# Sending the last batch's rows to the expert slots in one stream instead of in rounds of three

## The chip, the cores and the metric

The kernel runs on one core of one Trainium2 chip. The metric is the device time of one execution in microseconds (us), the median of several runs. Engines go by these names: PE is TensorE (PEld its weight loads), ACT is ScalarE, DVE is VectorE, POOL is GpSimd, SP is SyncE, which here only issues DMAs.

## What is computed

Four batches of 1024 tokens with 128 features go through four layers, each added to its input:

```
x = x + attn_a(layernorm(x))     # linear attention with exponential features, and an FFN
x = x + ffn(layernorm(x))        # mixture of experts (stages named m)
x = x + attn_b(layernorm(x))     # causal softmax attention, 16 heads of width 8
x = x + ffn(layernorm(x))        # the same mixture of experts again (stages named n)

def ffn(x):                      # 160 experts, the best 8 of each token, width 64
    top_w, top_idx = top_k(sigmoid(x @ router_w.T + bias), 8)
    h = silu(x @ w_gate[e].T)            # for each chosen expert e
    y = h @ w_down[e].T                  # weighted by top_w, summed over the 8
    return y + silu(x @ w_gate_shared.T) @ w_down_shared.T
```

## The kernel before, in words

A mixture layer works through DRAM. A router stage (`route`) finds for every token its 8 experts and for each of the 8 a slot. A slot is a row of the DRAM tensor `slots_in`. The rows are then sent there ("scattered"): one indirect DMA issued by POOL (line 859, in the class `Scatter`) sends 128 rows of 128 floats, for one tile of 128 tokens and one of the 8 choices. The 32 tiles of tokens are two halves of 16 tiles, each half with slots of its own, so a half needs 128 scatters. The expert stage (`experts`) reads the slots in order, computes, and writes `slots_out`. POOL then fetches the results back with indirect DMAs of the same size (line 884, class `Gather`), and DVE weighs and adds them.

The expert stage handles the two halves one after the other. A half has 52 groups of 8 blocks with 64 slots each. For one group, SP loads 256 KB of rows (line 1306), PE turns them (`psX`, line 1364, 4 matmuls), ACT copies them (`xT`, line 1409), PE does the first product (`psH`, line 1377, 16 matmuls), ACT squashes it (`hT`, line 1415), PE does the second product (`psY`, line 1388, 16 matmuls), ACT copies the result (`y`, line 1421, and adds 1 to the semaphore `y_ready`), and SP stores 256 KB (line 1311). PE's order is: `psH` of group n, `psX` of n+1, `psY` of n-1. ACT's is `hT` of n, `xT` of n+1, `y` of n-1. DVE copies expert weights into a ring of four buffers (`staged_w`, line 1446) for 32 of the 52 groups, each once `psY` has freed a buffer. Rows and results have rings of four buffers (`DEEP`).

The scatters of the first half are all done before the expert stage begins. Those of the second half are not: in the first expert stage (m) the 64 of the last batch are left, in the second (n) 70, which are those and the last 6 of the batch before. POOL sends them while PE and ACT compute the first half. The helper `spaced` ties them to the groups: three scatters, then a wait until ACT has written `y` of two more groups, then three more, and so on. The first three wait for nothing. When all are issued, POOL waits until they have landed and until the first half's results are stored, and then gathers the first half's results during the second half, again through `spaced`, two gathers for each group. SP begins to load the second half when the first half's stores are issued and the scatters of the second half have landed (semaphores `scattered`).

Of the kernel before, what the change touches and what calls it, by code (L numbers as in the profile page):

```python
# [41 lines left out]
EXPERTS, TOPK, INTER = 160, 8, 64  # L42
# [5 lines left out]
TPH = TILES // HALVES  # L48
# [816 lines left out]
class Gather:  # L865
# [12 lines left out]
    def issue(self, pool, count):  # L878
        for n in range(self.asked, self.asked + count):
            i, k = divmod(n, TOPK)  # L880
            t = self.first + i
            if k == 0 and i >= self.ring:
                pool.wait_ge(self.added, i - self.ring + 1)
            self.nc.gpsimd.indirect_dma_start(self.rows(i)[:, k, :], None, self.G.slots_out[t // TPH],  # L884
                                              bass.IndirectOffsetOnAxis(self.G.place[:, t, k:k + 1], 0)
                                              ).then_inc(self.gathered[i % self.ring], 16)
        self.asked += count
# [390 lines left out]
def experts(nc, stage, G, S, scatter, out=None):  # L1278
# [3 lines left out]
    with Memory(nc, stage) as m:  # L1282
# [10 lines left out]
        src, dst = ([s.rearrange("(g p j) d -> g p (j d)", p=P, j=TURNS) for s in slots] for slots in (G.slots_in, G.slots_out))  # L1293
        order = group_order()
        dynamic_at = [i for i, (_, d) in enumerate(order) if d is not None]
        rows_landed = [m.sem(f"rows_landed{i}") for i in range(DEEP)]
        stored = [m.sem(f"stored{i}") for i in range(DEEP)]
# [4 lines left out]
        @block.sync  # L1302
        def _(sp):
            def load(h, i):
                n = h * HALF_GROUPS + i
                sp.dma_start(rows[:, n % DEEP, :, :].rearrange(flat), src[h][order[i][0]]).then_inc(rows_landed[n % DEEP], 16)

            def store(h, i):
                n = h * HALF_GROUPS + i
                sp.wait_ge(y_ready, n + 1)  # L1310
                sp.dma_start(dst[h][order[i][0]], y[:, n % DEEP, :, :].rearrange(flat)).then_inc(stored[n % DEEP], 16)  # L1311

            for h in range(HALVES):
                for b in range(BPH * h, BPH * (h + 1)):
                    sp.wait_ge(S.scattered[b], 16 * TPB * TOPK)
                for i in range(DEEP):
                    load(h, i)
                for i in range(HALF_GROUPS):
                    if i + DEEP < HALF_GROUPS:
                        sp.wait_ge(x_turned, h * HALF_GROUPS + i + 1)  # L1320
                        load(h, i + DEEP)
                    store(h, i)
            for s in stored:
                sp.wait_ge(s, 16 * HALVES * HALF_GROUPS // DEEP)
            if out is not None:
                for b in range(BATCH):
                    sp.wait_ge(gather.added, TPB * (b + 1))
                    sp.dma_start(out[b].rearrange("(t p) d -> p t d", p=P), G.x[:, b, :, :]).then_inc(out_stored, 16)
                sp.wait_ge(out_stored, 16 * BATCH)

        @block.gpsimd
        def _(pool):
            def spaced(issue, count, first, transfers, groups):

                for n in range(0, count, transfers):
                    done = min(n // transfers * groups, HALF_GROUPS)
                    if done:
                        pool.wait_ge(y_ready, first + done)
                    issue(min(transfers, count - n))

            spaced(scatter, TPH * TOPK - scatter.sent, 0, 3, 2)
            for s in S.scattered[BPH:]:
                pool.wait_ge(s, 16 * TPB * TOPK)
            for s in stored:
                pool.wait_ge(s, 16 * HALF_GROUPS // DEEP)
            spaced(lambda count: gather.issue(pool, count), min(TPH, gather.tiles) * TOPK, HALF_GROUPS, 2, 1)
            if out is not None:
                for s in stored:
                    pool.wait_ge(s, 16 * HALVES * HALF_GROUPS // DEEP)
                gather.issue(pool, TPH * TOPK)  # L1350
# [84 lines left out]
        @block.vector  # L1435
        def _(dve):
            def stage_weights(h, d):
                _, e = nc.values_load_multi_w_load_instructions(
                    G.tile_expert[0:1, h, GROUP * d:GROUP * (d + 1)], engines=[mybir.EngineType.DVE], min_val=0, max_val=EXPERTS - 1,
                    skip_runtime_bounds_check_because="the plan clamps it to the last expert")  # L1440
                if d >= STAGED:
                    dve.wait_ge(down_done, h * HALF_GROUPS + dynamic_at[d - STAGED] + 1)
                elif h:
                    dve.wait_ge(down_done, (h - 1) * HALF_GROUPS + dynamic_at[DYN_GROUPS + d - STAGED] + 1)
                for j in range(GROUP):
                    last = nc.vector.tensor_copy(staged_w[:, d % STAGED, j, :],  # L1446
                                                 G.wgd[:].rearrange("p e i -> p (e i)")[:, bass.ds(e[j] * (INTER + DM), INTER + DM)])
                last.then_inc(staged, 1)

            for c in range(CHUNKS):  # L1450
                dve.wait_ge(S.weights_landed[c], 16)
            for d in range(DYN_GROUPS):
                stage_weights(0, d)
            done = 0
            for d in range(DYN_GROUPS):
                stage_weights(1, d)
                if d % 3 == 2 and d >= 2 * STAGED:
                    gather.add(dve, done)
                    done += 1
            for i in range(done, gather.tiles):  # L1460
                gather.add(dve, i)
# [974 lines left out]
```

## Time and profile before

| | us |
|---|---|
| median of 3 runs | 2910.31 (2908.22 to 2914.45) |
| the profiled execution | 2888.6 |
| its span, first to last instruction | 2887.3 |
| PE busy | 1992.7 (69%) |
| DVE busy | 1664.6 (58%) |
| POOL busy | 1306.3 (45%) |
| ACT busy | 1049.6 (36%) |
| scatters, line 859, 512 of them | 503.8 busy |
| gathers, line 884, 512 of them | 508.5 busy |

The profile is of one execution. Starts are counted from the beginning of the span. The two expert stages together are a little over a fifth of the span: stage m runs from about 983 to 1318 us, stage n from about 2328 to 2672 us.

### The profile page before, as it was taken

The page shows a single profiled execution, that of the slowest core. Times are in us where ns is not written, and L with a number is a line of the kernel's source. Part 1 is how long each engine was busy: PE and PEld are TensorE (multiplying, and loading weights), DVE is VectorE, ACT ScalarE, POOL GpSimd, SP SyncE. Part 2 cuts the span into 40 slices and gives each one's busy share as a digit, 9 for nine tenths or more (in the row PEclk, how much of TensorE's full clock was granted, in tenths as well). Part 3 has the DMA queues.
Part 4 walks back from the last instruction along what each step waited for, and adds up shares of the span by engine and source line. Part 5 has one row for each costly group of instructions (what it writes and reads, how often), then busy time and mean ns, then how long its engine had stood idle before and what let it go on. Part 6 is the DMA issues. An engine that isn't in the chain of part 4 may idle for free. (4 is left out here: it accounts for less than half of the span.)

```text
span 2887.3 us, 45561 instructions
## 1 busy us (share of the span) xinstructions
PE 1992.7 (69%) x15787; PEld 1142.0 (40%) x15787; DVE 1664.6 (58%) x4731; ACT 1049.6 (36%) x2016; POOL 1306.3 (45%) x1340
## 2 busy tenths in 40 slices
PE   5896696696696577664878788987988657766000
PEld 3455355255355355452333333433333335554000
DVE  5466566657567533355786787688785443245222
ACT  0253253253253245442355544434444234443000
POOL 0042265365465343554345540551454634356775
PEclk9898798698798599887687786787787679788555
DMA  9200000000003466664222121211200556565221
GB/s 378 86 1 4 15 15 23 22 18 20 28 16 158 154 209 202 193 189 144 53 70 65 50 64 25 60 54 43 58 32 23 207 191 209 189 194 179 72 60 46
DMA packets 132475, 275.69 MB, mean 95 GB/s; under 512 B 29411, under 2 KB 44387, under 8 KB 127891
## 3 DMA queue, kind: packets, MB, share of 16 engines
q1 hardware_dynamic: 99478, 205.60, 21.6%
q0 software_dynamic: 32768, 67.17, 7.7%
q8 instruction: 127, 2.08, 0.3%
q14 instruction: 102, 0.84, 0.1%
HBM read 146.34 MB, written 125.93 MB: 94 GB/s over the span
## 5 line engine op out<-in xcount | busy, mean ns | idle before, releaser
L859 POOL DMA_INDIRECT slots_in<-g_xs,g_place x512 | 503.8, 984 | 462.8 <-issue 119.3
L2199 ACT ACTIVATE b_pT<-b_psE 128x512 f32<-128x512 f32 (+3 forms) x768 | 326.6, 490 | 452.9 <-PE b_psE L2096 399.4
L1896 DVE TENSOR_REDUCE b_peak<-b_psM 128x1 f32<-128x512 f32 (+3 forms) x768 | 393.3, 550 | 145.0 <-PE b_psM L2084 88.2
L884 POOL DMA_INDIRECT r_xs<-slots_out,g_place x336 | 334.9, 997 | 226.8 <-ACT b_pT L2199 96.6
L2079 PE MATMUL b_psM<-b_kS,b_qS 72*128 72x512 bf16 (+3 forms) x640 | 242.4, 391 | 58.5 <-DVE b_peak L1896 33.0
L2096 PE MATMUL b_psE<-b_qS,b_kS 75*128 75x512 bf16 (+3 forms) x768 | 245.2, 397 | 44.5 <-ACT b_pT L2199 39.4
L884 POOL DMA_INDIRECT g_xs<-slots_out,g_place x176 | 173.6, 987 | 138.2 <-issue 46.4
L2108 PE MATMUL b_psV<-b_pT,b_vb 128*32 128x512 f32 (+3 forms) x1536 | 207.1, 622 | 23.9 <-POOL b_pT L2263 22.0
L1446 DVE COPY m_staged_w<-wgd 128x192 f32 x512 | 98.3, 264 | 203.6 <-PE m_psY L1388 113.0
L1446 DVE COPY n_staged_w<-wgd 128x192 f32 x512 | 97.1, 261 | 204.4 <-PE n_psY L1388 144.0
L2263 POOL TENSOR_SCALAR_AFFINE_SELECT b_pT<-b_pT 128x512 f32<-128x512 f32 x128 | 82.3, 643 | 206.9 <-ACT b_pT L2199 205.3
L2079 PEld LDWEIGHTS b_psM<-b_kS,b_qS 72*128 72x128 bf16 x640 | 69.8, 111 | 212.2 <-DVE b_peak L1896 131.6
L2096 PEld LDWEIGHTS b_psE<-b_qS,b_kS 75*128 75x128 bf16 x768 | 76.4, 111 | 156.7 <-ACT b_pT L2199 88.7
L2082 PE MATMUL b_psM<-b_kS,b_qS 72*128 72x128 bf16 x512 | 130.6, 255 | 8.3 <-DVE b_peak L1896 5.8
L2084 PE MATMUL b_psM<-b_mask_q,b_ident_bf 128*128 128x128 bf16 x512 | 131.4, 257 | 0.0
L417 PE MATMUL a__psA<-a_wk,a_xnT 128*128 128x512 f32 x128 | 67.8, 656 | 45.7 <-POOL a__v L378 45.7
L1364 PE MATMUL m_psX<-g_ident,m_rows 128*128 128x128 f32 x416 | 80.8, 325 | 25.8 <-issue 19.7
L1364 PE MATMUL n_psX<-g_ident,n_rows 128*128 128x128 f32 x416 | 80.9, 326 | 25.0 <-issue 18.9
L611 DVE TENSOR_REDUCE a__shift<-a__sq 128x16 f32<-128x1024 f32 x32 | 39.0, 1220 | 88.4 <-ACT a__sq L536 88.4
L385 POOL TENSOR_TENSOR a__fold<-a__sq 128x512 f32<-128x512 f32 x32 | 41.8, 1305 | 105.4 <-ACT a__sq L556 105.4
L1421 ACT ACTIVATE n_y<-n_psY 128x512 f32<-128x512 f32 x104 | 62.3, 601 | 72.8 <-DMA b_qS<-b_negp 40.2
L1409 ACT ACTIVATE m_xT<-m_psX 128x512 f32<-128x512 f32 x104 | 62.0, 597 | 69.3 <-PE m_psX L1364 62.4
(518 smaller groups left out, 4221.4 us busy)
## 6 DMA issues: line engine op xcount, KB each, us to landing
wgd<-in_w_gdT SPq DMA_DIRECT2D x8, 3840.0 KB, 23.0
slots_in<-g_xs SPq DMA_DIRECT2D x26, 1024.0 KB
m_rows<-slots_in SPq DMA_DIRECT2D x104, 256.0 KB
slots_out<-m_y SPq DMA_DIRECT2D x104, 256.0 KB
n_rows<-slots_in SPq DMA_DIRECT2D x104, 256.0 KB
slots_out<-n_y SPq DMA_DIRECT2D x104, 256.0 KB
b_qS<-q_parts SPq DMA_DIRECT2D x48, 192.0 KB
b_kS<-k_parts SPq DMA_DIRECT2D x48, 192.0 KB
```

The lines of the kernel that those rows point to most:

```text
L859: self.nc.gpsimd.indirect_dma_start(self.G.slots_in[self.h], bass.IndirectOffsetOnAxis(self.G.place[:, TPH * self.h + t, k:k + 1], 0), sel ...
L884: self.nc.gpsimd.indirect_dma_start(self.rows(i)[:, k, :], None, self.G.slots_out[t // TPH], bass.IndirectOffsetOnAxis(self.G.place[:, t, ...
L1364: last = nc.tensor.transpose(psX[:, n % 2, j * P:(j + 1) * P], rows[:, n % DEEP, j, :], G.ident[:])
L1446: last = nc.vector.tensor_copy(staged_w[:, d % STAGED, j, :], G.wgd[:].rearrange("p e i -> p (e i)")[:, bass.ds(e[j] * (INTER + DM), INTER ...
L1896: nc.vector.reduce_max(to, taking()[:, 0:size], AX.X).then_inc(m_taken, 1)
L2079: last = nc.tensor.matmul(ps[:, 0:edge], qS[0:STACK, g, h, qt * P:(qt + 1) * P], kS[0:STACK, g, h, kh * HALF:kh * HALF + edge], start=True ...
L2082: nc.tensor.matmul(ps[:, edge:n], qS[0:STACK, g, h, qt * P:(qt + 1) * P], kS[0:STACK, g, h, kh * HALF + edge:kh * HALF + n], start=True, s ...
L2084: last = nc.tensor.matmul(ps[:, edge:n], ident_bf[:], mask_q[:], start=False, stop=True)
L2096: nc.tensor.matmul(psE[:, j % BANKS, q0:HALF], kS[0:STACK + 3, g, h, kt * P:(kt + 1) * P], qS[0:STACK + 3, g, h, half * HALF + q0:(half + ...
L2108: last = nc.tensor.matmul(psV[32 * h:32 * h + 32, half, q0:HALF], vb[:, kt, g * HG + h, :], pT[:, e % KEPT, h, q0:HALF], start=(kt == 0), ...
L2199: nc.scalar.activation(pT[:, e % KEPT, h, q0:HALF], psE[:, j % BANKS, q0:HALF], ACT.Exp, scale=SCALE).then_inc(e_taken, 1)
L2263: nc.gpsimd.affine_select(out=tile, in_=tile, compare_op=ALU.is_ge, fill=0.0, base=0, pattern=[[0, HG], [1, P]], channel_multiplier=-1).th ...
```

## The change

The call of `spaced` for the scatters is replaced by one call of the scatter itself with the full count. POOL issues the remaining scatters one behind the other, with no wait on `y_ready` between them. Everything else stays, the paced gathers too.

```
-            spaced(scatter, TPH * TOPK - scatter.sent, 0, 3, 2)
+            scatter(TPH * TOPK - scatter.sent)
             for s in S.scattered[BPH:]:
                 pool.wait_ge(s, 16 * TPB * TOPK)
```

## Rows read from the trace of the kernel before

**Rows 1.** The page: busy time by engine, and the chain that ended last, by engine.
```profile
PE 1992.7 (69%) x15787; PEld 1142.0 (40%) x15787; DVE 1664.6 (58%) x4731; ACT 1049.6 (36%) x2016; POOL 1306.3 (45%) x1340
...
PE 7%; POOL 5%; issue 3%; ACT 1%; another core or an unknown queue 1%; DMA 0%; DVE 0%; POOLq 0%; SPq 0%; ACTq 0%; DVEq 0%
```

**Rows 2.** Windows, scatters alone: stretch, length, POOL busy (count), PE clock, DMA share, GB/s.
```profile
999.20:1119.30 120.10, 57.90 (x60) 0.91 0.65 208
1119.30:1138.00 18.70, 0.96 (x1) 1.00 0.68 229
...
2342.60:2474.80 132.20, 64.70 (x66) 0.91 0.65 211
```

**Rows 3.** Timeline, one round of three in stage n: start, length, engine, line [idle before].
```profile
2372.56 0.97 POOL L859 DMA_INDIRECT slots_in<-g_xs,g_place  x1 [2.40 <-ACT n_y L1421]
...
2373.05 0.67 PE L1388 MATMUL n_psY<-n_staged_w,n_hT 64*64 64x128 f32 x16
...
2373.80 0.69 PE L1377 MATMUL n_psH<-n_xT,n_staged_w 128*64 128x64 f32 x16
...
2375.11 0.97 POOL L859 DMA_INDIRECT slots_in<-g_xs,g_place  x1 [0.30 <-issue]
2375.34 0.60 ACT L1421 ACTIVATE n_y<-n_psY 128x512 f32<-128x512 f32 x1 [1.59 <-DMA b_qS<-b_negp]
...
2376.97 0.38 ACT L1415 ACTIVATE n_hT<-n_psH 128x256 f32<-128x256 f32 x1 [1.03 <-DMA b_kS<-k_parts]
...
2378.60 1.05 POOL L859 DMA_INDIRECT slots_in<-g_xs,g_place  x1 [2.52 <-ACT n_y L1421]
```

**Rows 4.** Timeline, ACT in stage m after its last scatter.
```profile
1120.81 0.60 ACT L1421 ACTIVATE m_y<-m_psY 128x512 f32<-128x512 f32 x1 [0.22 <-PE m_psY L1388]
...
1131.84 0.60 ACT L1421 ACTIVATE m_y<-m_psY 128x512 f32<-128x512 f32 x1
```

**Rows 5.** Timeline, where the first halves begin and end, stages m and n.
```profile
983.46 0.96 POOL L859 DMA_INDIRECT slots_in<-g_xs,g_place  x1 [19.49 <-POOLq L93]
...
1137.13 1.16 ACT L1421 ACTIVATE m_y<-m_psY 128x512 f32<-128x512 f32 x2 [0.23 <-PE m_psY L1388]
...
2328.83 0.97 POOL L859 DMA_INDIRECT slots_in<-g_xs,g_place  x1 [19.84 <-POOLq L93]
...
2332.03 1.11 PE L1364 MATMUL n_psX<-g_ident,n_rows 128*128 128x128 f32 x4 [18.87 <-issue]
...
2333.83 1.13 PE L1377 MATMUL n_psH<-n_xT,wgd 128*64 128x64 f32 x16 [0.69 <-ACT n_xT L1409]
...
2483.67 1.16 ACT L1421 ACTIVATE n_y<-n_psY 128x512 f32<-128x512 f32 x2 [0.23 <-PE n_psY L1388]
```

**Rows 6.** Windows, two cycles of gathers: gathers alone on POOL, then `n_y` alone on ACT.
```profile
2588.49:2595.10 6.61, 3.83 (x4) 1.00 0.64 201
2606.28:2616.49 10.21, 5.78 (x6) 0.82 0.49 149
...
2588.49:2595.10 6.61, 1.21 (x2) 1.00 0.64 201
2606.28:2616.49 10.21, 1.20 (x2) 0.82 0.49 149
```

**Rows 7.** Timeline, inside and behind the six gathers in a row.
```profile
2607.14 0.69 PE L1377 MATMUL n_psH<-n_xT,n_staged_w 128*64 128x64 f32 x16
...
2612.63 0.96 POOL L884 DMA_INDIRECT g_xs<-slots_out,g_place  x1 [0.30 <-issue]
2614.87 0.38 ACT L1415 ACTIVATE n_hT<-n_psH 128x256 f32<-128x256 f32 x1 [4.45 <-DMA b_kS<-k_parts]
```

**Rows 8.** Timeline, router stage of batch 3, between scatters sent back to back.
```profile
936.02 1.94 PE L1014 MATMUL m__ps_lo<-g_ident,g_xs 128*128 128x128 f32 x8 [16.39 <-DVE g_xs L1101]
936.16 0.96 POOL L859 DMA_INDIRECT slots_in<-g_xs,g_place  x1 [0.30 <-issue]
937.14 0.60 ACT L1078 ACTIVATE m__xnT<-m__ps_lo 128x512 f32<-128x512 f32 x1 [25.14 <-PE m__ps_lo L1014]
```

## Prediction, made before the changed kernel was run

> **What bounds the kernel now.** I read the page first, for who is busy and who is in the chain that ended last. No engine is busy throughout: PE has 69%, POOL 45%, and the chain as far as the profile can follow it is PE 7% and POOL 5% [rows 1]. So the answer depends on the stage, and the change touches only the first half of the two expert stages. Next I took the scatters by windows. Between the first scatter that waits for a group and the last, stage m has 60 scatters in 120.1 us and stage n 66 in 132.2 us [rows 2]. That is 20 and 22 rounds of three, two groups a round, so both stages run at 6.0 us a round, 3.0 us a group. POOL is busy for less than half of it (57.90 of 120.1) and waits for ACT the rest: POOL does not pace the groups by its own work, and DMA is at 0.65 of its time. The usual conclusion would be that PE and ACT set the pace and that the scatters are hidden.
>
> The timeline says otherwise. After stage m's last scatter, `y` starts at 1120.81 and, five groups later, at 1131.84, with loads and stores still going: 11.03 / 5 = 2.2 us a group [rows 4]. At full clock PE's three blocks of a group are about 0.66 us each (0.67 and 0.69 in the round shown [rows 3]), near 2.0 us together, so a group without scatters is set by PE and takes 2.0 to 2.2 us. I use **2.1 us**. With three scatters in every 6.04 us (2372.56 to 2378.60 [rows 3]) two groups take 6.04 instead of 4.2 us, so a round costs **1.84 us**, 0.61 us a scatter.
>
> Where it is lost can be seen in one round [rows 3]. `psY` is through at 2373.05 + 0.67 = 2373.72, but the `y` that needs it starts at 2375.34, 1.6 us later, with ACT idle. `psH` is through at 2374.49, and its `hT` starts at 2376.97, 2.5 us later and 0.9 us after the third scatter ended (2375.11 + 0.97 = 2376.08). The releasers printed there, DMAs of the attention layer, can't be meant: those tensors are out of use in this stage. What ACT waits for by the code is PE's semaphores. So while POOL issues scatters, PE's results reach ACT late. The trace shows that and not its mechanism.
>
> **The change, part by part.** It removes the waits on `y_ready`, 21 in stage m and 23 in stage n. It moves no other instruction: POOL has nothing queued behind the scatters except the waits for landing and storing and then the gathers, which need the first half's stores anyway. SP's wait for `scattered` before the second half is met earlier, and it was met in time before. It adds nothing. So nothing can be gained on POOL or SP, and what is left is how the same scatters, packed into one stream, slow PE and ACT.
>
> A scatter in a row takes 0.97 + 0.30 = 1.27 us [rows 3]. Stage m's 64 are a stream of 81 us, stage n's 70 one of 89 us. PE starts 3.2 us after the first scatter (2328.83 to 2332.03 [rows 5]), so three scatters cost nothing, now as then. That leaves 61 + 67 = 128 scatters beside running groups.
>
> What one of them costs in a stream is the number that decides. No scatter stream beside running groups is in the trace; the nearest rows are longer bursts of gathers in the second half, DMAs of the same size from the same queue. Four in a row: two groups in 6.61 us, 6.61 - 4.2 = 2.4 us lost, 0.60 each. Six in a row: two groups in 10.21 us, 6.0 us lost, 1.0 each [rows 6]. From three to six in a row the loss rises from 1.84 to 6.0 us, 1.39 us for each added one, which is more than the 1.27 us that it lasts. In the long burst `psH` was through at 2607.83 and `hT` started at 2614.87, 7 us later and 1.3 us after the burst's end (2612.63 + 0.96) [rows 7]. So the gap behind a burst is when PE's results get through, and a stream has no gap. Bounds for the loss per scatter are 0.60 us (as in short bursts) and 1.27 us (groups stand still). I take **1.05 us**, near the six in a row, a little above as there is no pause in 61.
>
> The Trainium skill says the opposite of these rows: in "SBUF — State Buffer", section "Who interferes with whom", PE and ACT never wait on anyone and DMA never contends with a compute engine. By that rule a scatter costs the groups nothing, neither in rounds nor in a stream.
>
> Stage m: the stream ends 81 us after its first scatter, and results get through 1 us later. PE has had 82 - 3 = 79 us, less 61 x 1.05 = 64 us, so 15 us, 7 groups. The other 45 take 45 x 2.1 = 94.5 us. I add 2 us for the last group's way through ACT and for a PE clock that comes back from its lower level (16 `psH` matmuls take 1.13 us at the start of a stage [rows 5] and 0.69 at full clock). Sum: 82 + 94.5 + 2 = 178.5 us. Before it is 983.46 to 1138.29, 154.8 us [rows 5]. **Plus 23.7 us.**
>
> Stage n: 89 + 1 = 90 us, PE has 87 - 67 x 1.05 = 16.5 us, 8 groups; the other 44 take 92.4 us; 90 + 92.4 + 2 = 184.4 us. Before it is 2328.83 to 2484.83, 156.0 us [rows 5]. **Plus 28.4 us.**
>
> The second halves, with the gathers, stay as they are, only later. The sum is +52 us on the profiled execution's 2888.6 us, 2941 us. The median shown, 2910.3 us, is 21.7 us above that execution; I put the same difference on it: **2962 us**.
>
> **The rivals.**
>
> *The same loss per scatter.* Each scatter costs 0.61 us, wherever it stands. For it: four in a row cost 0.60 each, like three. Against it: the six. Then stage m has done 20 groups by the stream's end (79 - 61 x 0.61 = 42 us) and stage n 22, and the end comes at 82 + 32 x 2.1 + 2 = 151 and 90 + 30 x 2.1 + 2 = 155 us, 4 and 1 us under before: about 2905 us, a measured "no change" (the bound of what can be told from no change is 0.2%, 5.8 us).
>
> *The scatters cost nothing.* Something else makes the rounds 6 us long, and taking the waits out changes nothing: 2910 us. For it: POOL is far from busy, and in the router stage PE's first four transposes are through near 936.99 (half of the 1.94 us) and ACT starts on them at 937.14, 0.15 us later, in the middle of scatters sent back to back [rows 8]. So a stream alone doesn't hold PE back; the groups' many small matmuls or SP's loads must have part in it. Against it: the pace turns from 3.0 to 2.2 us a group at the last scatter, in the same stage. The rule cited above from the Trainium skill, "SBUF — State Buffer", would give this case.
>
> *A loss per burst, faster.* The loss is charged once for every burst, not for every scatter, as when PE's signals are held up only at a burst's start. It decides if a stream costs less than about 0.6 us a scatter. Three and four in a row cost 1.84 and 2.4 us, which is not far from a constant; the six speak against it. With 42 rounds gone and two bursts in their place, 40 x 1.84 = 74 us go: 2836 us. Half-way to it, at 0.5 us a scatter, it is 128 x 0.11 = 14 us under the equal case, near 2890 us.
>
> *Standstill.* Each scatter costs its whole 1.27 us: 82 + 52 x 2.1 + 2 = 193 and 201 us, +38 and +45, 2993 us; with 2.2 us a group another 10 us, 3003 us.
>
> **How the numbers follow.** Slower by my mechanism, from 0.75 us a scatter to standstill: 0.69. The same loss per scatter or none: 0.13. Faster, by the loss per burst or a part of it: 0.18. A loss of 0.75 is 38 us under the sum at 1.05, so the likeliest case has 2924 to 3003 us of its own, its middle 2962. The range takes in the equal cases and the half-way fast one and stops short of the pure loss per burst: 2888 to 3000 us. Slower by over 0.2%: 0.70, within 0.2%: 0.11, faster: 0.19.
>
> **What would show each step.** Right: 64 and 70 scatters back to back at 1.27 us from 983 and 2329 us; some 7 or 8 `y` while they last, `hT` starting several us after its `psH`; low DMA share and probably a lower PE clock there; afterwards 2.1 us a group; the first halves 178 and 184 us long. Wrong: more than 20 `y` beside each stream (the loss is smaller), or a pace after the stream far from 2.1 us, as when the loads at 256 KB in and out for every group become the bound. Wrong in another way: DVE's copies of weights could stretch scatters beyond 1.27 us, and a stream of 90 us would grow.

## The result and the profile after

The changed kernel is slower. Its four executions took 2989.42 to 3004.28 us, median 2998.59; the four of the kernel before 2908.22 to 2915.16, median 2912.38. The ratio is 1.0278, 95% interval 1.0254 to 1.0301, or +86 us. I had said 2962 us, in a range of 2888 to 3000. The sign was right, and so was the mechanism, that scatters in a stream hold back PE's results. The size was the one that I had priced as "standstill" (2993 us).

The page of the changed kernel (execution of 2989.42 us), busy time and the chain by engine, to hold against [rows 1]:

```profile
PE 1984.4 (66%) x15787; PEld 1133.0 (38%) x15787; DVE 1664.4 (56%) x4731; ACT 1055.4 (35%) x2016; POOL 1297.1 (43%) x1340
...
PE 5%; POOL 5%; another core or an unknown queue 5%; issue 2%; ACT 1%; DMA 1%; DVE 0%; POOLq 0%; SPq 0%; ACTq 0%; DVEq 0%
```

Every engine is busy for as long as before, within 10 us. Between the two profiled executions the span grew by 100.8 us, all of it time in which the engines are idle, and the page alone doesn't say where. The windows do. First stage m's first half in three stretches with all engines (the stream, the time from its end to the first `y`, the rest), then `m_y` alone on ACT in the same stretches, then stage n's stream, scatters alone on POOL. The columns are length, busy (count) by engine, PE clock, DMA share, GB/s:

```profile
984.92:1065.41 80.49, 9.02 (x78) 6.48 (x79) 6.74 (x32) 2.56 (x5) 61.28 (x64) 0.52 0.20 68
1065.41:1074.95 9.54, 2.65 (x11) 1.30 (x11) 0.00 (x0) 0.00 (x0) 0.00 (x1) 0.50 0.02 7
1074.95:1178.48 103.53, 95.41 (x1787) 70.50 (x1786) 45.61 (x253) 79.16 (x151) 0.00 (x0) 0.97 0.75 248
...
984.92:1065.41 80.49, 0.00 (x0) 0.52 0.20 68
1065.41:1074.95 9.54, 0.00 (x0) 0.50 0.02 7
1074.95:1178.48 103.53, 31.07 (x52) 0.97 0.75 248
...
2377.63:2466.45 88.82, 67.79 (x70) 0.50 0.20 66
```

PE does 78 matmuls in 80 us where it needs 36 for each group, and there is no `y` at all in the stream nor in the 9.5 us behind it. Then all 52 follow in 103.5 us. Stage n repeats it. The next rows show ACT in m from the start, and the two ends of the first halves, to hold against [rows 4, 5]:

```profile
989.38 0.60 ACT L1409 ACTIVATE m_xT<-m_psX 128x512 f32<-128x512 f32 x1 [35.25 <-issue]
1002.02 0.38 ACT L1415 ACTIVATE m_hT<-m_psH 128x256 f32<-128x256 f32 x1 [12.04 <-remote]
1005.57 0.60 ACT L1409 ACTIVATE m_xT<-m_psX 128x512 f32<-128x512 f32 x1 [3.17 <-DMA a_proj<-in_projT]
1045.50 0.38 ACT L1415 ACTIVATE m_hT<-m_psH 128x256 f32<-128x256 f32 x1 [39.33 <-remote]
1056.70 0.60 ACT L1409 ACTIVATE m_xT<-m_psX 128x512 f32<-128x512 f32 x1 [10.82 <-DMA a_proj<-in_projT]
1074.95 0.60 ACT L1421 ACTIVATE m_y<-m_psY 128x512 f32<-128x512 f32 x1 [17.65 <-remote]
...
1177.17 1.16 ACT L1421 ACTIVATE m_y<-m_psY 128x512 f32<-128x512 f32 x2 [0.23 <-PE m_psY L1388]
...
2578.90 1.16 ACT L1421 ACTIVATE n_y<-n_psY 128x512 f32<-128x512 f32 x2 [0.23 <-PE n_psY L1388]
```

So m's first half lasts from 984.92 to 1178.33, 193.4 us in place of 154.8, and n's from 2377.63 to 2580.06, 202.4 us in place of 156.0. That is 38.6 + 46.4 = 85 us, the whole difference of the medians. The second halves are 6.3 and 5.3 us longer in this trace as well; in the runs below, which leave the gathers as they are, they vary by as much without the stream, so I don't put that on the change.

The same stage on PE shows how it stands still. These rows are from the first half's third group, at the stream's end:

```profile
1057.35 1.12 PE L1377 MATMUL m_psH<-m_xT,wgd 128*64 128x64 f32 x16 [43.00 <-issue]
...
1061.59 0.37 PE L1364 MATMUL m_psX<-g_ident,m_rows 128*128 128x128 f32 x1 [3.12 <-issue]
...
1063.69 0.37 PE L1364 MATMUL m_psX<-g_ident,m_rows 128*128 128x128 f32 x1 [1.73 <-issue]
1064.46 0.95 POOL L859 DMA_INDIRECT slots_in<-g_xs,g_place  x1 [0.31 <-issue]
```

The four transposes of `psX`, which at this clock are otherwise one piece of 1.12 us, come one at a time, two or more us apart, and the profile gives nothing that they wait for. The 9.5 us behind the stream are of the same kind: a backlog of PE that drains after the last scatter.

But most of the time goes by between PE's records and its signals. The second group's `psH` and the first group's `psY` are recorded early in the stream:

```profile
1006.22 1.12 PE L1377 MATMUL m_psH<-m_xT,wgd 128*64 128x64 f32 x16 [14.03 <-issue]
...
1008.32 1.15 PE L1388 MATMUL m_psY<-wgd,m_hT 64*64 64x128 f32 x14
```

The `hT` that needs this `psH` starts at 1045.50, 38 us after the recorded end, and the `y` that needs this `psY` at 1074.95. PE's records run ahead: 34 matmuls and 34 weight loads within 3.3 us from 1006.22 on, and only then singly. So the 78 matmuls above are not results that ACT could use. Whether the array really did the work at the recorded time and only the signal was late, or the work itself was, the profile can't tell, as it models the ends of matmuls.

### The profile page after: what moved, and what is told of

It reads as the page before. It is cut to its first block and busy times, and to the rows that moved or that the text cites. A ratio compares the mean times of both kernels' runs of the same rounds, so it can differ in the third digit from the quotient of the medians.

```text
span 2988.1 us, 45561 instructions
## 1 busy us (share of the span) xinstructions
PE 1984.4 (66%) x15787; PEld 1133.0 (38%) x15787; DVE 1664.4 (56%) x4731; ACT 1055.4 (35%) x2016; POOL 1297.1 (43%) x1340
## 3 DMA queue, kind: packets, MB, share of 16 engines
q0 software_dynamic: 32768, 67.17, 7.5%
## 5 line engine op out<-in xcount | busy, mean ns | idle before, releaser
L1364 PE MATMUL n_psX<-g_ident,n_rows 128*128 128x128 f32 x416 | 80.9, 323 | 38.6 <-DMA n_rows<-slots_in 26.9
L1409 ACT ACTIVATE n_xT<-n_psX 128x512 f32<-128x512 f32 x104 | 62.1, 597 | 83.0 <-issue 33.9
```

Source lines behind the costliest of these rows:

```text
L1364: last = nc.tensor.transpose(psX[:, n % 2, j * P:(j + 1) * P], rows[:, n % DEEP, j, :], G.ident[:])
L1409: nc.scalar.activation(xT[:, n % 2, :], psX[:, n % 2, :], ACT.Copy).then_inc(xT_ready, 1)
```

## The experiments

Theory A: while GpSimd sends indirect DMAs back to back, PE's instructions and its signals hardly get through, so a burst costs its own length, less what the rings of two and four buffers cover (no run changed a ring, so that they are what covers it is argued). The rivals are those of the prediction, and others as they came up. Ratios are to the kernel before, taken in the same set of runs.

**The stream in one stage.** `stage == "m"` streams, n keeps its rounds:

```
+            if stage == "m":
+                scatter(TPH * TOPK - scatter.sent)
             spaced(scatter, TPH * TOPK - scatter.sent, 0, 3, 2)
```

> The stream in stage m alone; stage n keeps its rounds of three. Theory A, standstill: the groups get nothing done while scatters are sent back to back, so a stream costs its own length, and the two stages are independent. The first half of m grew from 154.8 to 193.6 us in the changed kernel's trace, so this run should be 39 us above the kernel before (ratio about 1.013), with stage n's first half back at 156 us. Rival B, a cost that builds up over the run (a PE clock that stays low, DMA queues that stay full): the sum over the two stages is not additive and this run is well away from +39, by 10 us or more.

Measured: 2951.4 against 2920.6 us, ratio 1.0106 (1.0078 to 1.0134), +31 us, 8 us less than expected. The interval just reaches the expected +39, and rival B asked for a distance of 10 us or more. Stage m from just before its first scatter to its last `y`:

```profile
984.60:1178.50 193.90, 107.22 (x1872) 78.17 (x1872) 52.12 (x284) 81.78 (x156) 61.48 (x64) 0.75 0.49 161
```

193.9 us, as in the changed kernel. So the cost of m's stream doesn't depend on n's: it is made inside the stage.

**No scatter beside the groups.**

```
-            spaced(scatter, TPH * TOPK - scatter.sent, 0, 3, 2)
+            pool.wait_ge(y_ready, HALF_GROUPS)
+            scatter(TPH * TOPK - scatter.sent)
```

> No scatter beside the first halves: all 64 and 70 are sent after y of group 52, so they lie beside nothing. This gives the pace of undisturbed groups, and it tells standstill from a partial loss. Theory A, standstill: 52 groups at 2.03 us and 5 us at the start and end are 111 us, then 82 and 89 us of stream before the second half can be loaded: 193 and 200 us, the same as the changed kernel, +86 us on the kernel before (ratio 1.028 to 1.033). My prediction's term, 1.05 us lost per scatter, had 7 and 8 groups done beside each stream; then this order should be 15 + 16 = 31 us slower than the changed kernel, ratio about 1.04.

Measured: 2997.1 against 2920.6 us, ratio 1.0249 (1.0218 to 1.0279). That is just under the expected 1.028, and its interval overlaps the changed kernel's. The groups of m, first `y` to last, all engines, and then the two streams behind the first halves, scatters alone:

```profile
994.96:1098.75 103.79, 94.26 (x1812) 69.56 (x1812) 45.42 (x251) 79.41 (x151) 0.00 (x0) 1.00 0.76 248
...
1099.09:1180.50 81.41, 61.27 (x64) 0.51 0.17 58
2501.60:2590.00 88.40, 66.79 (x70) 0.51 0.16 55
```

This is the run that decides between my number and the standstill. Putting the stream beside the groups or behind them comes to the same time, so nothing of the two overlaps. With 1.05 us lost per scatter, this order would have been some 31 us slower than the changed kernel. It also gives the undisturbed pace: 103.8 / 51 = 2.03 us a group, at full clock. Before, the same stretch took 143 us (995.26, the start of the first `y`, to 1138.29), so the rounds of three had cost 39 us in m already.

**One at a time, and two.** After the first three scatters, each waits for a PE step of the groups, spread evenly over the first half:

```
+            scatter(3)
+            left = TPH * TOPK - scatter.sent
+            for n in range(left):
+                i, third = divmod((n + 1) * 3 * (HALF_GROUPS - 1) // left, 3)
+                done, value = ((up_done, i + 1), (x_turned, min(i + 2, HALF_GROUPS)), (down_done, i))[third]
+                if value:
+                    pool.wait_ge(done, value)
+                scatter(1)
```

> Same scatters, but after the first three each is sent alone, after every second or third of the groups' three PE steps (about one each 1.7 to 2.6 us). Theory A, the hold lasts as long as the burst and PE's results get through in the gap, while the rings of two hide some 2 us of it (three cost 1.84 us, four 2.4, six 6.0): a lone scatter of 1.27 us is hidden or nearly so, the first halves come to some 115 to 130 us, and the run is 50 to 80 us faster than the kernel before (ratio 0.972 to 0.983). Rival C, a cost per scatter whatever the burst, 0.6 us: same as before within 10 us. Rival D, each pause and start has a cost of its own (the loss per burst): 61 bursts in place of 20 make it slower, by 40 x 1.84 us or more per stage.

Measured: 2865.3 against 2920.6 us, ratio 0.9814 (0.9787 to 0.9841). The pairs are the same code with half as many steps and `scatter(2)`:

> After the first three, the scatters go in pairs, evenly spaced over the PE steps of the first halves. Theory A, a burst of length L costs L less about 1.8 us until PE's clock falls as well (one costs 0.2 to 0.3 us, three in a row cost 1.98 us, six in a row 8.3 us with the clock's part): a pair of 2.5 us costs 0.7 to 1.1 us, the first halves lie 8 to 18 us under the kernel before each, ratio 0.988 to 0.994, between the single ones (0.981) and the threes. Rival C, a cost per scatter whatever the burst: like the single ones or like the threes.

Measured: 2893.2 against 2913.9 us, ratio 0.9935 (0.9913 to 0.9956). Scatters alone on POOL, from the first `y` to the last, m and n; first the single ones, in a second fence the pairs:

```profile
996.19:1112.03 115.84, 57.81 (x60) 1.00 0.80 256
2322.68:2445.17 122.49, 63.28 (x65) 0.98 0.75 245
```

```profile
996.89:1133.14 136.25, 57.55 (x61) 0.99 0.67 218
2345.53:2481.70 136.17, 65.22 (x67) 0.98 0.69 221
```

The same number of scatters as in the rounds of three: singles take 12 and 19 us over the undisturbed 103.8, pairs 32, threes 39 and 41. Rivals C (a cost per scatter) and D (a cost per burst) both fall.

**Six in a row.** `spaced(..., 0, 6, 4)` in place of `0, 3, 2`:

> Same number of scatters a group as before, but six in a row for four groups. Theory A, the groups stand still for a burst's length less some 1.8 us that the rings hide (three last 3.8 us and cost 6.04 - 2 x 2.03 = 1.98 us): six last 7.6 us and cost 5.8 us; 10 to 11 rounds a stage cost 21 us more than the 20 to 22 rounds of three, together +43 us, ratio 1.015. Rival C, a cost per scatter whatever the burst: no change. Rival D, a cost per burst: half as many bursts, 40 us faster.

Measured: 2978.5 against 2900.8 us, ratio 1.0275 (1.0235 to 1.0316), +78 us where I expected +43. A cycle, scatters alone, and then ACT in it. The last of the six scatters is busy from 1037.81 to 1038.77.

```profile
1031.49:1048.08 16.59, 5.75 (x6) 0.69 0.48 152
```

```profile
1038.67 0.39 ACT L1415 ACTIVATE m_hT<-m_psH 128x256 f32<-128x256 f32 x1 [5.21 <-issue]
...
1040.60 0.59 ACT L1421 ACTIVATE m_y<-m_psY 128x512 f32<-128x512 f32 x1
...
1044.05 0.60 ACT L1421 ACTIVATE m_y<-m_psY 128x512 f32<-128x512 f32 x1 [0.49 <-PE m_psY L1388]
...
1047.21 0.60 ACT L1421 ACTIVATE m_y<-m_psY 128x512 f32<-128x512 f32 x1 [0.49 <-PE m_psY L1388]
```

So `hT`, at 1038.67, starts as the sixth scatter ends: held for the burst, as theory A has it. What my sum lacked stands behind it. The groups after the burst take 3.5 and 3.2 us instead of 2.03, as the mean granted clock of the cycle is 0.69: PE has no matmul from 1035.30 to 1040.75, and from 1037 to 1044 the granted clock is 0.50, the lower level (1.2 GHz), so the first groups behind the burst run at it. A cycle loses 16.59 - 4 x 2.03 = 8.5 us, which is more than the 7.6 us that its scatters last. I had expected 5.8 us. So six in a row is about as bad as the whole stream.

**What of a scatter does it?** Four kernels, each of one execution, so that their times are rough and the rows carry the argument. In the first, the scatters of the streams send rows of 32 floats instead of 128 (`self.rows[:, t, 0:self.wide]`); the other three quarters of the data are left out:

```
+            scatter.wide = 32
             scatter(TPH * TOPK - scatter.sent)
```

> The changed kernel with the streamed scatters of both expert stages moving rows of 32 floats instead of 128, a quarter of the bytes (three quarters of those rows are left out and they land elsewhere in the slots). Rows per scatter and scatters stay. Theory A with the reason in the issuing (what holds PE is each scatter's processing by GpSimd and its 128 rows, not the bytes): the stream stays 81 us long, m_y of the first half again starts 90 us after the first scatter, time as the changed kernel, 2990 to 3005 us. Rival E, the bytes moved hold PE's results back: most of the groups get through, 10 or more y in the stream, and the run is at 2950 us or below.

Measured: 2986.6 us, the kernel before 2900.8. ACT in stage m:

```profile
1071.70 0.60 ACT L1422 ACTIVATE m_y<-m_psY 128x512 f32<-128x512 f32 x1 [23.24 <-remote]
```

No `y` before 1071.70, 9 us after the stream's end: a quarter of the bytes holds PE as long. Not the bytes.

The second has 64 rows to a scatter instead of 128 (`self.rows[0:64, t, :]` and `place[0:64, ...]`) and leaves the other half out:

> The changed kernel with 64 rows instead of 128 in each scatter of the two streams (the other half of those rows is left out). Theory I, beside a stream PE gets one instruction through for each scatter, whatever its size: 64 scatters, so again hT and xT of 2 to 3 groups beside the stream and y only after it; if the scatters follow each other faster, the stream and the stretch without y shrink with them. Theory J, what counts is rows: a PE instruction gets through for each 128 rows, so the groups are held for less per scatter, PE's signals come at twice the rate per scatter or some y falls in the stream.

Measured: 3006.4 us, before 2913.9. A scatter with half the rows is busy for 0.90 instead of 0.96 us and comes every 1.21 us, and ACT shows the same picture:

```profile
1015.07 0.60 ACT L1410 ACTIVATE m_xT<-m_psX 128x512 f32<-128x512 f32 x1 [9.42 <-issue]
1059.87 0.38 ACT L1416 ACTIVATE m_hT<-m_psH 128x256 f32<-128x256 f32 x1 [44.20 <-remote]
...
1073.98 0.60 ACT L1422 ACTIVATE m_y<-m_psY 128x512 f32<-128x512 f32 x1 [4.41 <-remote]
```

Not the number of rows either (theory J falls). What stays the same is one scatter every 1.2 to 1.3 us.

The third keeps GpSimd busy without DMAs:

```
+            for _ in range(TPH * TOPK - scatter.sent):
+                nc.gpsimd.memset(filled[:], 0.0)
+                nc.gpsimd.drain()
+            pool.wait_ge(y_ready, HALF_GROUPS)
             scatter(TPH * TOPK - scatter.sent)
```

> GpSimd runs 64 and 70 memory fills of 128x768 floats, each followed by a drain, at the start of the expert stages, and the scatters are sent after group 52. What is compared is the first halves with those of the run where GpSimd does nothing there (103 us from the first to the last y). Theory A1, it is DMA issuing that holds PE: first halves 103 us as there, also while the fills last, time about 2997 us. Rival F, GpSimd's being busy is enough: the groups stand still while the fills last, and the time rises by the length of both series of fills.

The fourth has plain DMAs from GpSimd's queue in their place:

```
+            for i in range(TPH * TOPK // 2):
+                nc.gpsimd.dma_start(G.slots_out[1][P * i:P * (i + 1), :],
+                                    scatter.rows[:, TPH // 2 + i // TOPK, :]).then_inc(plain, 16)
+            pool.wait_ge(plain, 16 * (TPH * TOPK // 2))
+            pool.wait_ge(y_ready, HALF_GROUPS)
             scatter(TPH * TOPK - scatter.sent)
```

> GpSimd issues 64 plain DMAs of 128 rows of 128 floats (the same size and source as the scatters, rows in a fixed order, to a part of slots_out that isn't in use) back to back at the start of both expert stages, and the scatters after group 52. Theory A1, any DMA that GpSimd issues holds PE: the groups stand still while they last, y of the first half starts after them, and the run is longer than 2997 us by the two series' length. Rival G, only the indirect form does it: y flows at 2.0 to 2.1 us a group from the start, time about 2997 us.

Measured: 3000.0 us with the fills, 2987.7 us with the plain DMAs, before 2900.8. The expectations name 2997 us for no effect, which was measured where the kernel before took 2920.6. At its ratio of 1.0249 no effect would be 2973 us here, so both runs are a little above it, by 27 and 15 us. `m_y` alone on ACT while the fills last, and in a second fence while plain DMAs last (the last of them ends at 1015.98, and two thirds of the 64 come after the first `y`):

```profile
993.34:1041.30 47.96, 12.56 (x21) 0.96 0.70 226
```

```profile
993.48:1020.00 26.52, 6.58 (x11) 0.98 0.96 316
```

21 groups in 48 us beside the fills (2.3 us a group), and beside the plain DMAs ten `y` start from 994.00 to 1015.11 (2.35), although these DMAs come every 0.53 us (64 in 34.06 us), twice as often as the scatters, and the DMA share is 0.96. Beside a stream of scatters there was none. Both cost something: the first halves are 111.0 and 111.5 us long with the fills and 107.6 and 106.8 with the plain DMAs, from first to last `y`, instead of 103.8 and 103.2. But neither GpSimd's being busy nor transfers from its queue hold PE back by more than that. It is the indirect form. The packets don't tell the forms apart: GpSimd's queue moves 32768 for 1024 scatters and gathers, 32 each, and the 128 plain DMAs add 4096, also 32 each.

**Fewer PE instructions.** The two products of a group with 2 wide calls each. They use the weights of a group's first experts only, so part of the computation is left out. The first product (the second is changed alike):

```
-                for j in range(GROUP):
+                for j in range(2):
                     w = (...)[:, 0:INTER]
...
+                    last = nc.tensor.matmul(psH[INTER * j:INTER * (j + 1), n % 2, 0:GROUP // 2 * ROWS], w,
+                                            xT[:, n % 2, HALF // 2 * j:HALF // 2 * (j + 1)], start=True, stop=True)
```

> The changed kernel (streams in both stages) with the two products of a group made by 2 wide calls each in place of 8 (4 recorded matmuls in place of 16): the wide calls use the weights of the first experts only, so part of the computation is left out. A group has 12 recorded matmuls and 12 weight loads in place of 36 and 36; the scatters and SP's transfers are the same. Theory A1, beside a stream PE is held for time, whatever it does: again 2 to 3 groups' worth of steps beside a stream of 80 us (the changed kernel had xT of 3 groups and 78 matmuls there). Theory A2, beside a stream PE gets through a fixed number of instructions (78 matmuls and 79 loads in 80 us): 6 or 7 groups. Theory A3, it is the high rate of small matmuls that collides with the scatters, and at a third of the rate nothing is lost: 25 groups or more beside the stream.

Measured: 2956.2 us, before 2920.6. ACT in the second part of m's stream, where each of PE's three steps now has 4 recorded matmuls and 4 weight loads:

```profile
1016.19 0.38 ACT L1414 ACTIVATE m_hT<-m_psH 128x256 f32<-128x256 f32 x1 [7.86 <-remote]
1026.69 0.60 ACT L1408 ACTIVATE m_xT<-m_psX 128x512 f32<-128x512 f32 x1 [10.12 <-DMA a_proj<-in_projT]
1037.89 0.60 ACT L1420 ACTIVATE m_y<-m_psY 128x512 f32<-128x512 f32 x1 [10.60 <-remote]
1049.12 0.38 ACT L1414 ACTIVATE m_hT<-m_psH 128x256 f32<-128x256 f32 x1 [10.63 <-remote]
```

From 1016.19 on there is a signal every 10.5 to 11.2 us, always behind 8 PE instructions: 1.3 to 1.4 us for each. In the changed kernel `xT` at 1005.57 to `hT` at 1045.50 spans the 32 instructions of a `psH`, 39.9 us, 1.25 us each, and `hT` to `xT` at 1056.70 the 8 of a `psX`, 11.2 us. With 64 rows it is 44.8 us and 1.4 us for the `psH`. A scatter comes every 1.21 to 1.27 us. So in the later part of a stream PE gets about one instruction through for each scatter, and at that rate an original group with 36 matmuls and 36 loads would need some 90 us.

The rate isn't there from the start. The changed kernel's first `psH`, also 32 instructions, was through 12.6 us after the first `xT` began in m (989.38 to 1002.02), 0.4 us each, and 7.6 us after it in n; n's second `psH` took 22.5 us, 0.7 each. Here the signals before 1016.19 came 5.6 to 8.5 us apart. So the hold grows over the first 20 to 40 us of a stream. Theory A2 (a fixed number of instructions) fits the later intervals; its count of 6 or 7 groups was too high, as 5 `xT` and 2 `y` fell in m's stream (5 and 3 in n's), since it was taken from matmuls recorded and not from results that were through.

**The gathers too.** On top of `one_at_a_time`, in the second halves:

```
+            for n in range(min(TPH, gather.tiles) * TOPK):
+                i = min((n + 1) // 2, HALF_GROUPS - 1)
+                if n:
+                    pool.wait_ge(*((down_done, HALF_GROUPS + i), (up_done, HALF_GROUPS + i + 1))[n % 2])
+                gather.issue(pool, 1)
```

> The scatters one at a time as in the run one_at_a_time (ratio 0.981), and the second halves' gathers one at a time as well, one when a group's first product is done and one when its second is, in place of two in a row for each group. Theory A, a burst costs its length less what the rings hide, and single ones hardly anything: pairs cost the second halves 3.3 us a group against 2.03; singles could bring that to about 2.6, which is two gathers of 1.27 us; the second halves shorten by up to 30 us each, ratio 0.96. Rival H, two singles a group leave a gap of only some 0.7 us between them, which is too short for PE's results to get through, and they act like a long burst: second halves as long as before or longer, ratio 0.98 or above.

Measured: 2838.5 against 2913.9 us, ratio 0.9746 (0.9727 to 0.9766), the fastest version of this study. Between both expectations: the second halves are 162 and 168 us in place of 169.5 and 175.6 before (174.6 and 184.0 in the trace of `one_at_a_time`), windows from first to last `y`, all engines; and in the second fence a pair of the timeline:

```profile
1124.59:1286.88 162.29, 110.98 (x1816) 79.10 (x1812) 79.56 (x281) 73.01 (x151) 90.23 (x94) 0.93 0.64 197
2454.14:2621.64 167.50, 113.44 (x1816) 81.67 (x1812) 80.47 (x284) 72.84 (x151) 99.00 (x102) 0.92 0.63 194
```

```profile
1153.25 0.60 ACT L1432 ACTIVATE m_y<-m_psY 128x512 f32<-128x512 f32 x1 [1.73 <-remote]
1153.48 0.95 POOL L884 DMA_INDIRECT r_xs<-slots_out,g_place  x1 [1.04 <-remote]
...
1154.74 0.94 POOL L884 DMA_INDIRECT r_xs<-slots_out,g_place  x1 [0.30 <-issue]
```

The waits make pairs again (0.30 us apart): 37 of the bursts in m's second half are pairs, as if both of PE's signals were held and came out together. Rival H was right about that. What is gone are the fours: before, the same 94 gathers were 19 pairs and 14 fours, now there are two bursts of more than three. The granted clock is 0.93 and 0.92 instead of 0.85 and 0.83.

**A gap without a tie to the groups.** The changed kernel's idea, with a fill and a drain behind each scatter:

```
+            for n in range(TPH * TOPK - scatter.sent):
+                scatter(1)
+                nc.gpsimd.memset(filled[:], 0.0)
+                nc.gpsimd.drain()
```

> As in the changed kernel no scatter waits for a group, but after each scatter GpSimd runs a fill of 128x384 floats and a drain. Fills alone, twice as wide, followed each other every 0.93 us and cost the groups next to nothing, so this puts a gap of about half a us on top of the 0.3 us between scatters: one scatter each 1.7 to 1.9 us, whatever the groups do, 64 of them in 109 to 122 us. Theory A, what PE needs is a gap behind each scatter, not a tie to the groups: y flows at 2.2 to 2.6 us a group from the start, the first halves are 115 to 135 us long, ratio 0.975 to 0.99. Rival K, the gap must fall where PE has just ended a step, as the waits on its semaphores make it: without that the scatters hit the groups at any place, the groups are held and the run is slower than the kernel before.

Measured: 2947.0 us, ratio 1.0825 (1.0762 to 1.0887). But the kernel before took 2721.6 us in this set, on a fourth chip, and this number can't be read with the others. The expectation failed on its own term as well: with the drain behind each, a scatter came every 3.0 to 5.5 us, 3.6 on average, 64 of them lasted until 1197.6, and the second half had to wait for them from 1088.9 on. POOL near the start, then all engines in m, the groups of the first half and of the second:

```profile
984.19 0.96 POOL L859 DMA_INDIRECT slots_in<-g_xs,g_place  x1 [2.16 <-issue]
985.15 0.43 POOL L1344 MEMSET m_filled<- 128x384 f32 x1
988.19 0.96 POOL L859 DMA_INDIRECT slots_in<-g_xs,g_place  x1 [2.60 <-issue]
...
983.11:1088.64 105.53, 95.73 (x1816) 70.56 (x1812) 52.55 (x249) 79.21 (x151) 34.85 (x49) 0.99 0.80 259
1209.33:1326.00 116.67, 97.39 (x1817) 71.35 (x1812) 75.61 (x275) 79.20 (x151) 87.94 (x91) 0.98 0.85 271
```

It doesn't test what it was meant for: whether a gap is enough when it isn't tied to the groups (rival K) stays open. What it shows instead is told at the end.

## Why the prediction was right in kind and short in size

- **The same scatters slow the groups.** Right. Before, the rounds already cost 39 us in m over the undisturbed 103.8 us.
- **1.27 us a scatter, streams of 81 and 89 us, PE's start 3.2 us after the first.** Right: 80.5 and 88.8 us, and 988.23 - 984.92 = 3.3 us. DVE didn't stretch them.
- **"I take 1.05 us" per scatter: the step that failed.** From PE's start to the last `y` the changed kernel's m takes 190.1 us, and undisturbed groups 8 us to the first `y` and 103.8 us after it, 111.8. The difference, 78.3 us over 61 scatters, is 1.28 us each, in n 88.7 over 67, 1.32 us. I had both bounds and took a value between them by the six gathers in a row (1.0 each), a little above. That row was a poor neighbour: of a short burst the first 1 to 2 us cost nothing (by the costs below), and beyond that every scatter costs its full length. The long burst is nearer to the slope from three to six, 1.39 us, which I had worked out and not used.
- **7 and 8 groups beside the streams.** Wrong: none, and three `xT`. My sum let PE finish groups in what was left over; with about one PE instruction per scatter in most of the stream there is nothing left over.
- **"Results get through 1 us later".** 9.5 us in m. In n 4.0, but the second `y` comes another 6.5 us later (2470.42 and 2476.92). I read it as a backlog that builds up in a stream and not in a short burst, so that those rows could not show it.
- **2.1 us a group afterwards, 2 us for the last group and the clock.** 2.03 us, that is 3 us less for a half; the clock was 0.50 in the stream and the first groups ran at it.
- **Sum.** Predicted 178.5 and 184.4 us, measured 193.4 and 202.4. Of the missing 14.9 us in m, 8.0 are the later release (90.0 us to the first `y` instead of 82) and 8.9 the groups still to do (103.4 us instead of 94.5), less the 2 us that I had added. In n it is 2.8 + 17.2 - 2 = 18.0 us.
- **The rivals.** Standstill was the case that came, and my 2993 us for it is 0.2% off. The same loss per scatter, and a loss per burst, are refuted by one, two, three and six in a row. In [rows 3] and [rows 6] the costs of three and four looked linear, 0.61 and 0.60 us a scatter; two in a row (0.5 each) and one (0.2 to 0.3) show that they are not.
- **The shape of the cost**, from these runs (length from first `y` to last `y` less 103.8 us, over the number of bursts as scatters divided by burst length, m / n): one 0.2 / 0.3 us, two 1.1 / 1.0, three 1.9 / 1.8, six 7.6 / 7.4, 61 of them 78. For instance 115.84 - 103.79 = 12.05 over 60.

What the groups lose is shown by runs (held for the burst, only for the indirect form, about one PE instruction per scatter once a stream has lasted some tens of us). Which part of the chip PE and the indirect DMAs share is not. That the signal comes up to 38 us behind the recorded end, and that the intervals fit a count in which weight loads stand beside matmuls, speaks for something in the path of PE's instructions or their completions and against the arrays and memories; this is argued, not shown.

## What to carry to other kernels

Before indirect DMAs are put beside small matmuls, look in the trace for the time between PE's end and the start of what it releases; if it grows while GpSimd sends them, overlap is not free however low GpSimd's busy share is. Then the order matters more than the number: single ones with a gap cost 0.2 to 0.3 us here, six in a row (with the lower clock behind them) no less than their length. A cost that must be taken from neighbours by size should be taken from the slope at the long end, not from the mean, since a fixed part of each burst costs nothing.

## What was not expected of the hardware

**On one chip the hold was not there.** Four sets of runs lay on four chips. On three, the kernel before took 2920.6, 2900.8 and 2913.9 us. On the fourth it took 2721.6 us. Which chip the main result comes from isn't known; its 2912.4 us are like the three. `fixed_gaps` ran there with unchanged gathers, and its rows show PE's results getting through in the middle of gathers sent back to back:

```profile
1239.34 0.95 POOL L884 DMA_INDIRECT r_xs<-slots_out,g_place  x1 [0.30 <-issue]
...
1240.07 0.38 ACT L1419 ACTIVATE m_hT<-m_psH 128x256 f32<-128x256 f32 x1 [0.16 <-PE m_psH L1381]
...
1240.59 0.95 POOL L884 DMA_INDIRECT r_xs<-slots_out,g_place  x1 [0.30 <-issue]
```

ACT is idle for 0.16 us before `hT`, where in [rows 7] it was 4.45 us. The second halves take 117 and 120 us instead of 170 and 176. The sum fits: 53 + 56 us less in the second halves, and 38 + 42 us if the first halves of the kernel before ran like these (105.5 and 102.9 us instead of 143.0 and 144.8), are 189 us, and 2912 - 2722 is 190. The kernel before has no trace from there, so that last step is argued. The changed kernel was not run there; by this its stream should cost the groups little on such a chip. There was one set on each chip, so whether the difference lies in the chip or in a state it was in stays open.

"PE and ACT never wait on anyone", says the Trainium skill in "SBUF — State Buffer", section "Who interferes with whom". The fourth chip comes near to it (first halves of 105.5 and 102.9 us), and so do the fills and the plain DMAs on another (2.3 us a group). The scatters and gathers on the three chips do not: no `y` in the 90 us from the stream's start, and in [rows 7] an `hT` that is 7 us late. That section is on the ports of the SBUF memory; whether the hold lies there, no run shows.

**A drain behind an indirect DMA is slow.** With a fill of twice the width a fill and its drain took 0.93 us; behind a scatter, 1.6 to 4.1 us passed between the fill's end and the next scatter, 2.2 on average.
